# Gate and up products in plain fp32 instead of three fp32r passes, with the one-hot weights on GpSimd

## The reference

```python
# Mamba: x [4,128,256] -> layer norm over the channels -> 4 chunks of 32 channels
xz = x @ in_proj.T                      # 32 -> 2 x 64
xc = silu(causal_conv4(xi) + conv_b)    # along the 256 positions
dt, B, C = split(xc @ x_proj.T)         # 2, 16 and 16 columns
dt = softplus(dt @ dt_proj.T + dt_b)
for t in range(256):                    # state h: 64 x 16 per chunk and image
    h = exp(dt_t * A) * h + (dt_t * x_t) * B_t
    y_t = (h * C_t).sum(states)
y = ((y + xc * D) * silu(z)) @ out_proj.T + skip * chunk
x1 = x + layer_norm(y) @ proj.T + proj_b
# experts: per token t = layer_norm(x1), 128 channels
logits = t @ router.T                   # 16 experts
w = softmax(top2(logits))               # zero for the other 14
out = x1 + sum_e w_e * ((silu(t @ gate_e) * (t @ up_e)) @ down_e)   # 128 -> 256 -> 128
```

## Time and profile before

| | |
|---|---|
| median of 3 runs | 349.1 us (345.41 to 350.11) |
| profiled execution | 346.35 us |
| its span | 344.4 us |
| mean granted clock of TensorE | 0.94 |

### The profile page before, as it was taken

One profiled execution on the slowest core, in us unless ns is written; L12 is line 12 of the kernel. 1 busy time (PEld: TensorE's weight loads), 2 busy tenths in 40 slices (PEclk: granted clock), 3 DMA queues, 4 the chain that ended last, 5 costly groups with the idle time before them and its releaser, 6 DMA issues. The chain is left out here.

```text
span 344.4 us, 4597 instructions
## 1 busy us (share of the span) xinstructions
PE 289.8 (84%) x1456; PEld 212.3 (62%) x1456; DVE 282.1 (82%) x447; ACT 171.4 (50%) x256; POOL 198.5 (58%) x183
## 2 busy tenths in 40 slices
PE   8967659977984788997688889976989889999996
PEld 6734513323431366776476677764779789889885
DVE  2899498999799488999979999998887568666763
ACT  3799155552553236785234376933434673343331
POOL 4869998886463064987758678874771121221220
PEclk9998965998999699999969999988899999999999
DMA  8903964343342001222111312210000000000000
GB/s 275 337 2 109 260 184 139 124 132 112 115 136 75 22 32 62 72 80 89 58 36 51 105 48 73 84 61 0 2 0 18 0 2 0 1 17 0 2 1 17
DMA packets 17112, 25.23 MB, mean 73 GB/s; under 512 B 2496, under 2 KB 7616, under 8 KB 17088
## 3 DMA queue, kind: packets, MB, share of 16 engines
q1 hardware_dynamic: 16944, 24.39, 22.3%
q10 hardware_dynamic: 144, 0.55, 0.5%
HBM read 24.14 MB, written 0.79 MB: 72 GB/s over the span
## 5 line engine op out<-in xcount | busy, mean ns | idle before, releaser
L505 ACT ACTIVATE dt<-bank,cst 128x512 f32<-128x512 f32 x64 | 44.0, 688 | 101.8 <-PE bank L902 101.6
L324 POOL TENSOR_TENSOR ring<-dtx,ring 128x512 f32<-128x512 f32 x64 | 82.1, 1290 | 19.2 <-DVE ring L634 18.7
L634 DVE TENSOR_TENSOR_SCAN ring<-bank,ring 128x512 f32<-128x512 f32 x64 | 77.8, 1215 | 7.6 <-POOL ring L324 5.4
L336 POOL TENSOR_TENSOR xs_lo<-xc,xs_hi 128x512 fp32r<-128x512 f32 x32 | 40.9, 1279 | 72.6 <-ACT xs_hi L499 72.6
L460 ACT ACTIVATE bank<-dt,cst,A 128x510 f32<-128x510 f32 x64 | 49.7, 777 | 47.5 <-DVE ring L634 46.5
L900 PE MATMUL bank<-xs_hi,Wu_hi 128*128 128x256 f32 x128 | 41.9, 327 | 23.5 <-DVE zs L734 12.4
L330 POOL TENSOR_TENSOR y<-y,ring 128x512 f32<-128x512 f32 x30 | 38.7, 1291 | 35.5 <-DVE ring L645 35.5
L724 DVE SCALAR_TENSOR_TENSOR dt<-dt,bank 128x512 f32<-128x512 f32 x64 | 43.6, 682 | 15.7 <-ACT dt L505 15.5
L900 PE MATMUL bank<-tn_hi,Wg_hi 128*128 128x256 f32 x128 | 48.9, 382 | 0.0
L775 PE MATMUL bank<-C_rows,sel 64*128 64x512 f32 x64 | 34.2, 535 | 17.0 <-DVE ring L645 15.5
L645 DVE TENSOR_TENSOR ring<-ring,bank 128x512 f32<-128x512 f32 x62 | 41.6, 671 | 6.6 <-PE bank L775 6.5
(11 more groups left out here) (135 smaller groups left out, 515.5 us busy)
## 6 DMA issues: line engine op xcount, KB each, us to landing
ring<-B_far SPq DMA_DIRECT2D x128, 128.0 KB, 3.0
stage_buf<-up_w SPq DMA_DIRECT2D x8, 256.0 KB, 6.4
ring<-gate_w SPq DMA_DIRECT2D x6, 256.0 KB, 5.3
par<-params ACTq DMA_DIRECT2D x1, 533.5 KB, 4.2
X<-x SPq DMA_DIRECT2D x2, 256.0 KB, 4.7
xm<-gate_w SPq DMA_DIRECT2D x2, 256.0 KB, 5.8
out<-X SPq DMA_DIRECT2D x4, 128.0 KB, 1.7
B_far<-B_rows SPq DMA_DIRECT2D x4, 64.0 KB, 2.9
```

The lines of the kernel that those rows point to most:

```text
L324: g.tensor_tensor(u[:, k % 3], dtx[:, k // NS, :], Bs[:, k % B_RING], ALU.mult).then_inc(S["u_r"], 1)
L336: g.tensor_tensor(xs_lo[:, pr % 2, :], xs, xs_hi[:, pr % 2, :].bitcast(F32), ALU.subtract)\
L505: a.activation(th[n % 2], bank[gate_bank(n)][:], ACT.Tanh, scale=0.5, bias=zero).then_inc(S["th_r"], 1)
L634: v.tensor_tensor_scan(h[:, k % 3], bank[da_bank(k)][:], u[:, k % 3], 0.0, ALU.mult, ALU.add)\
```

## The change

Gate and up become one plain fp32 product each per half, from weights that arrive unsplit in two transfers; every rounding and residual of weights and tokens goes. The scaled tokens get two buffers of their own. The work of i = 16 moves from VectorE to GpSimd, except for the reciprocal; the cast of the indices goes with it, and ScalarE makes the sum 1 + e. The tables place it: GpSimd does i = 16 at offset 12 (group 0) and 11 (the others), and TensorE transposes at offset 13 instead of 12 in group 0. At the start, VectorE and ScalarE take group 0's softplus ahead of the B and C rows of the other groups, whose last ones are now made beside scans 0 and 1; the first B rows are sent for group 0 alone, and a filler of eight small products goes.

```diff
-BESIDE_STEPS = {"DVE": {1: 0, 5: 5, 6: 7, 9: 12, 10: 14, 11: 15, 12: 16, 14: 19},
+BESIDE_STEPS = {"DVE": {1: 0, 5: 5, 6: 7, 9: 12, 10: 14, 12: 16, 14: 19},
+                "POOL": {12: 16},
+                "PE": {2: 1, 3: 3, 5: 6, 6: 8, 7: 10, 9: 13, 13: 17},
...
-            for c in range(CHUNKS_W):
-                w, es = weight_chunk(c)
-                sp.dma_start(stage(c), (gate_w, up_w)[w][es].rearrange("e h f -> h e f"))\
-                    .then_inc(S[f"w_in{c}"], 16)
+            sp.dma_start(Wg[:], gate_w.rearrange("e h f -> h e f")).then_inc(S["wg_in"], 16)
+            sp.dma_start(Wu[:], up_w.rearrange("e h f -> h e f")).then_inc(S["wu_in"], 16)
...
-            for c in range(1, CHUNKS_W):
-                split_rest(c)
...
-            def split_scaled(pr):
-                pool.wait_ge(S["xsh_r"], pr + 1)
-                if pr >= 2:
-                    pool.wait_ge(S["up_r"], 2 * (pr - 1))
-                g.tensor_tensor(xs_lo[:, pr % 2, :], xs, xs_hi[:, pr % 2, :].bitcast(F32), ALU.subtract)\
-                    .then_inc(S["xsl_r"], 1)
+            def back(i, b):
+                if i == 16:
+                    pool.wait_ge(S["topi_r"], BLK * (b + 1))
+                    g.tensor_copy(topf[:], topi[:, :, 0:2]).then_inc(S["topf_r"], 1)
+                    pool.wait_ge(S["topf_r"], b + 1)
+                    pool.wait_ge(S["w0_r"], b + 1)
+                    g.tensor_tensor(w01[:, :, 1:2], e1[:], w01[:, :, 0:1], ALU.mult).then_inc(S["w1_r"], 1)
+                    pool.wait_ge(S["w1_r"], b + 1)
+                    for j in range(2):
+                        for i_ in range(BLK):
+                            g.tensor_scalar(oh[b][:, j, i_, :], iota_e[:, i_, :], topf[:, i_, j:j + 1],
+                                            w01[:, i_, j:j + 1], ALU.is_equal, ALU.mult).then_inc(S["ow_r"], 1)
+                    pool.wait_ge(S["ow_r"], 2 * BLK * (b + 1))
+                    for j in range(2):
+                        g.tensor_tensor(cpad[:, :, 32 * j:32 * j + E], oh[b][:, 0], oh[b][:, 1], ALU.add)\
+                            .then_inc(S["ce_r"], 1)
...
                 if i == 15:
                     act.wait_ge(S["dif_r"], b + 1)
                     a.activation(e1[:], e1[:], ACT.Exp, bias=zero).then_inc(S["ex_r"], 1)
+                    act.wait_ge(S["ex_r"], b + 1)
+                    a.activation(w01[:, :, 0:1], e1[:], ACT.Copy, bias=1.0).then_inc(S["sum_r"], 1)
...
             def scale_tokens(pr):
                 b = 2 * pr // E
                 dve.wait_ge(S["ceb_r"], 2 * pr + 2)
-                if pr:
-                    dve.wait_ge(S["xsl_r"], pr)
+                if pr >= 2:
+                    dve.wait_ge(S["up_r"], 2 * (pr - 1))
...
             def spread_c(k):
                 if before(c_bank, k):
                     pe.wait_ge(S["hc_r"], before(c_bank, k))
+                elif k:
+                    pe.wait_ge(S["bcl_r"], BATCH)
+                    pe.wait_ge(S["brow_r"], BATCH)
...
-            pe.wait_ge(S["bcl_r"], BATCH)
+            pe.wait_ge(S["bcl_r"], 3)
             spread_c(0)
-            keep_warm(8, 7)
...
-            def product(o, w_hi, w_lo, hi, lo, name, first=True, last=True):
-                t.matmul(o, w_hi, hi, start=first, stop=False)
-                t.matmul(o, w_hi, lo, start=False, stop=False)
-                o_ = t.matmul(o, w_lo, hi, start=False, stop=last)
...
                 for f in range(FH):
-                    ws = slice(f * P, (f + 1) * P)
-                    product(bank[up_bank(n)][:, f * T:(f + 1) * T], W_hi[1][:, e, ws], W_lo[1][:, e, ws],
-                            xs_hi[:, pr % 2, ts], xs_lo[:, pr % 2, ts], "up_r" if f == FH - 1 else None)
+                    o = t.matmul(bank[up_bank(n)][:, f * T:(f + 1) * T], Wu[:, e, f * P:(f + 1) * P],
+                                 xs[:, pr % 2, ts], start=True, stop=True)
+                o.then_inc(S["up_r"], 1)
```

More of the change, by code:

```diff
@@ L130, in build @@
         CE = sb("CE", [P, BATCH, T], F32R)
-        with ExitStack() as stage_ctx:
-            stage_buf = stage_ctx.enter_context(nc.sbuf_tensor("stage_buf", [P, 8, N], F32))
-        tn_hi = sb("tn_hi", [P, BATCH, T], F32R)
-        tn_lo = sb("tn_lo", [P, BATCH, T], F32R)
-        xs_hi = sb("xs_hi", [P, 2, N], F32R)
-        xs_lo = sb("xs_lo", [P, 2, N], F32R)
+        xs = sb("xs", [P, 2, N])
         with ExitStack() as scan_ctx:
@@ L160, in build @@
         tn = xm
-        stages = [ring[:, 3 + i, :] for i in range(6)] \
-            + [xm[:, 2 * i:2 * i + 2, :].rearrange("p b t -> p (b t)") for i in range(2)] \
-            + [stage_buf[:, i, :] for i in range(8)]
-        def stage(c):
-            return stages[c].rearrange("p (e f) -> p e f", f=F)
-        def weight_chunk(c):
-            return c * WCH // E, slice(c * WCH % E, c * WCH % E + WCH)
         def half(buf, i):
@@ L240, in put_result @@
                 sp.dma_start(out[b], X[:, b, :]).then_inc(S["out_d"], 16)
-            for b in range(2):
-                put_rows(b)
+            put_rows(0)
             for k in range(B_RING):
@@ L347, in _ @@
                     scan_source(gr)
-            split_scaled(0)
+                back(*chain("POOL", k))
             for n in range(ITEMS):
                 k = step_at(n)
-                if n % 2 == 1 and n + 1 < ITEMS:
-                    split_scaled((n + 1) // 2)
                 if k + 1 < STEPS:
@@ L426, in _ @@
                 present_tap(b)
-            for c in (DVE_W, DVE_W + 1):
-                round_weights(c)
             for b in (0, 1):
@@ L447, in _ @@
             quadratic_2(0)
-            for b in (2, 3):
+            for b in (0, 1):
                 round_bc(b)
@@ L466, in _ @@
                 decay(k)
+                round_bc(2 + k)
             def back(i, b, tables):
@@ L526, in _ @@
                     decay(k + 1)
-                if n % 2 == 0 and n // 2 + 1 < ITEMS // 2:
-                    round_scaled(n // 2 + 1)
                 back(*chain("ACT", k), True)
@@ L624, in _ @@
             v.tensor_tensor(dt[:, 0, :], dt[:, 0, :], y[:, 0, :], ALU.add).then_inc(S["dt_r"], 1)
-            for b in (2, 3):
-                bc_rows(b)
-                bc_rest(b)
+            for d in range(2):
+                bc_rest(d)
+                if d:
+                    bc_rows(d)
+                    dve.wait_ge(S["brow_r"], d + 1)
+                dve.wait_ge(S["bcl_r"], d + 1)
+                edge = bank[d][:].rearrange("p (q t) -> p q t", t=T)[:, :, 0:1]
+                v.memset(edge, 0.0).then_inc(S["da0"], 1)
+            bc_rows(2)
             def scan(k):
@@ L741, in _ @@
                 scan(k)
+                if k == 0:
+                    bc_rest(2)
+                if k == 1:
+                    bc_rows(3)
+                    bc_rest(3)
                 if k:
@@ L917, in gate @@
                 for f in range(FH):
-                    ws = slice(f * P, (f + 1) * P)
-                    product(bank[gate_bank(n)][:, f * T:(f + 1) * T], W_hi[0][:, e, ws], W_lo[0][:, e, ws],
-                            tn_hi[:, b, :], tn_lo[:, b, :], "g_r" if f == FH - 1 else None)
+                    o = t.matmul(bank[gate_bank(n)][:, f * T:(f + 1) * T], Wg[:, e, f * P:(f + 1) * P], tn[:, b, :],
+                                 start=True, stop=True)
+                o.then_inc(S["g_r"], 1)
             def up(n):
```

118 lines of the change are left out of this document (22 added, 96 removed).

## The result

The changed kernel takes 336.26 us (median of 4 runs, 332.98 to 337.62), the kernel before 347.77 us beside it (4 runs). The ratio is 0.9655, 95% interval 0.9547 to 0.9763: faster, by 11.5 us. The forecast was 335, with a range of 326 to 343. Marks are start times in us from the span's start, read from the timelines: scan 28 is the last scan before group 0's one-hot weights are made, "item n" is its `hidden` product on VectorE.

The account below looks back on a forecast made before the run. VectorE was taken to bound scans beside experts, TensorE nearly the experts alone. Terms -5.2, -2.3, -8.5 and +3.8 sum to -12.2 us against 346.35, giving 334.2; the forecast was 335, range 326 to 343.

Parts of the forecast that it names:

- The product: Gate and up on TensorE: each rises from 0.69 to 0.86 us per item, as plain fp32 like down.
- Start: Start and first scans: scan 0's wait for GpSimd goes, a wait behind the down weights replaces it; scan 4 -5.2 us.
- End of the scans alone: Group 0's one-hot seam up to item 0: work leaves VectorE, later transposes give some back; -2.3 us, ends -4.5 and +1.
- Beside the experts: Scans 32 to 63 beside experts 0 to 31: VectorE loses work, GpSimd and TensorE cost some; -8.5 us, ends -12.5 and -3.
- TensorE becomes the bound beside the scans: Rival, chance 0.20: third stage gains 3 instead of 8.5 us, the last loses 5 instead of 3.8; 341 us.
- Experts alone: Experts 32 to 63 after the scans: dearer products fill TensorE's idle time; +3.8 us, ends +1.3 and +10.7.
- GpSimd's small operations: Eight one-hot operations per group on GpSimd beside the scans: 1.6 us per group, ends 1.2 and 3.6.
- the dear case: Rival, chance 0.08: GpSimd's small operations at scan steps 28, 43 and 59 cost about 11 us per group; 362 us.

Follow-up runs that it names:

- the changed kernel's second profile: The changed kernel run again with no edit and profiled once more; median 335.57 us, ratio 0.9649 to the kernel before.
- The trial at the old price: Changed kernel with gate and up as six single-pass matmuls of a ready rounded tile, real weights and tokens left out; 326.86 us, 0.9396 of the kernel before.

## Why the prediction was right

The forecast holds: -12.2 us foretold, -8.9 in the first profiled pair (346.35 to 337.47), -13.1 against the changed kernel's second profile, -11.5 in the medians. The stages that carry the gain are the ones foretold, the start and the stage beside the experts. That the sum comes so near is partly luck. One term was 4.2 us too good and another 2.4 too dear, and the sum has nothing for scans 4 to 22, which moved by +1.3 us in the first profile and -2.9 in the second with the clock. By its terms:

- **The product, right.** 0.86 us per item for each of gate and up. The four-pass rule of the Trainium skill (FP8 and Floating Point Precision, TensorE Precision Notes) agrees in direction: 0.43 us per product against 0.345 for three passes. That is 1.25 times as much, where four passes at the rate of the three would be 1.33.
- **Start, right** (-5.2; scan 4 moved by -4.3). Scan 0 came at 35.2, 0.2 past the 34 to 35, and the old wait turned into one for a transfer, 6.49 us. Issuing the down weights earlier removed it. Of the missing 0.9 us they can account for all: they were issued at 32.75 and took 11.3 us, where I had about 32 and 10.3.
- **End of the scans alone, wrong in sign** (-2.3 foretold). This is the mis-sized term. Of the 2.3, 1.2 are the residual and the cast ahead of scan 28, and they came: scan 22 to 28 took 13.44 us before and 12.15 after. The other 1.1 lie behind scan 28, and there 18.70 us became 21.89, +3.2. From scan 28 to 29 the one-hot work is gone, -2.0, as foretold. From 29 to 30 the scan input behind GpSimd's block costs +2.3, which I had counted only for the stage beside the experts. From 30 to 31 the late transposes cost +3.7, where I had 1.9. From there to item 0 it is -0.8. In the second profile the stretch took 21.69 us, so this is no accident of the first. With the early transposes it was 18.37 us, 3.3 less. The clock, taken as 0, fell in this stretch from 0.82 to 0.69, but among the trials it changed the stretch by a few tenths at most.
- **Beside the experts, right in sum, not in its parts** (-8.5; measured -9.0). VectorE's work fell by 10.2 us (123.42 to 113.21), as foretold. But I had 9.4 of it for the one-hot work with its cast and 0.8 for the tokens' residual. The trial with the one-hot on VectorE gives 5.7 for the move. The other 4.5 were gone without it: the residual, the sum 1 + e that ScalarE now makes (2.5 us for two groups), and small operations that got cheaper or dearer in another order. So the match of 10.2 is partly luck. The idle time beside it rose by 1.3 us, where I had 1.7. The five gaps of 2.1 us went, as foretold, and GpSimd's block cost two waits of 1.2 us, 2.4 where I had 1.6. The rest, waits for TensorE and ScalarE, grew by 1.0, where I had +2.2 for TensorE. The trial at the old price gives 0.4 net for that, about 2.9 by the estimate without its stretches at half clock. The rival "TensorE becomes the bound beside the scans" asked for a gain of only 3 us in this stage, and it was 9.0.
- **Experts alone, right in kind, too dear** (+3.8; +2.0 between the same marks, +1.4 from item 32 to 63). From up(32) at 241.49 to the end of up(63) at 330.32 are 88.8 us, against 88.1 of work: the 2.5 us of idle that I kept for the table switches were 0.7. The product costs 8.4 us from item 32 to 63, and the splits' removal gives 7.0 back (86.3 to 79.3 at the product's old price), most of it idle time of TensorE (5.1 to 0.4).
- **GpSimd's small operations**: about 2.5 us per group, inside my ends of 1.2 and 3.6; the dear case did not come.
- Start to item 0 is -7.5 by my terms and -1.2 in the first profile, -5.5 in the second (122.38 to 116.93); the 4.3 between the two is TensorE at half clock in scans 16 to 22.

What the change is worth by parts, beside the scans: the dear product +0.4 net, the splits' and the one-hot's removal -9.4 (131.2 to 121.9), of which 4.2 the one-hot's move. No one part stands for the whole. The dear product with the splits kept loses 8.2 us; with the splits gone it costs 8.4 us in the last stage, where their removal gives 7.0 back, and the gain is made in the stages before.

## What to carry to other kernels

A dearer operation on one engine has to be priced stage by stage, together with the work that it replaces on others. Here the same product cost 8.4 us in the stage of experts alone, where TensorE sets the pace, and 0.4 net in the one beside the scans. Where an operation is moved to an engine that another chain waits for, look at both its followers, the consumer by its place in the order and what is queued behind it; here the consumer's place alone cost 3.4 us, beside a gain of 11.5. Where two profiles differ by more than the effect, compare them stage by stage with the clock beside it before reading anything from the span. A cheaper operation can be paid for with a lower clock, as the product at its old price was in its one profile (0.97 beside the scans, against 1.00).
